# Square 32x32 tiles for s, full-height products with wq, and every B product inside U, in a 12-layer linear-attention kernel

## The reference

```python
for i in range(N_LAYER):                       # 12 layers, 16 heads of 8 channels
    qkv = x @ Wqkv[i].T + bqkv[i]
    q, k, v = jnp.split(qkv, 3, axis=-1)       # then reshaped to (B, H, T, D)
    att = jnp.einsum('bhqd,bhkd->bhqk', q, k) * scale
    y = jnp.einsum('bhqk,bhkd->bhqd', att, v)
    x = y.transpose(0, 2, 1, 3).reshape(B, T, C) @ Wproj[i].T + bproj[i] + x
# around it
x = _layernorm(x + _L0_attn_ref(x, ...))
x = _layernorm(x + _L0_ffn_ref(x, w_gate, w_up, w_down))
```

## Time and profile before

| | |
|---|---|
| median of 3 runs | 310.84 us |
| lowest and highest | 309.97, 310.84 us |
| the profiled execution | span 308.2 us from its first to its last instruction |
| TensorE matmul busy | 302.1 us, 98% |
| TensorE weight loads busy | 283.8 us, 92% |
| VectorE, ScalarE, GpSimd busy | 216.9, 192.0, 133.8 us |
| granted TensorE clock, mean | 0.999 |

### The profile page before, as it was taken

One profiled execution on the slowest core, in us unless ns is written; L12 is line 12 of the kernel. 1 busy time (PEld: TensorE's weight loads), 2 busy tenths in 40 slices (PEclk: granted clock), 3 DMA queues, 4 the chain that ended last, 5 costly groups with the idle time before them and its releaser, 6 DMA issues.

```text
span 308.2 us, 9599 instructions
## 1 busy us (share of the span) xinstructions
PE 302.1 (98%) x4010; PEld 283.8 (92%) x4010; DVE 216.9 (70%) x651; ACT 192.0 (62%) x459; POOL 133.8 (43%) x142
## 2 busy tenths in 40 slices
PE   8999999999999999999999999999999999999994
PEld 8989999899998998989989999899998889999983
DVE  0477586676876768758677587676765997888874
ACT  3458667686585675865758668577586276444451
POOL 3064180480723806418045072360634663655533
PEclk9999999999999999999999999999999999999999
DMA  7603003030030210300203002020000000121112
GB/s 265 265 2 113 6 6 109 4 113 2 2 115 3 74 43 4 113 4 10 105 5 113 2 3 79 4 75 6 5 0 2 2 2 0 37 64 41 34 35 72
DMA packets 8908, 14.96 MB, mean 49 GB/s; under 512 B 800, under 2 KB 5280, under 8 KB 8864
## 3 DMA queue, kind: packets, MB, share of 16 engines
q1 hardware_dynamic: 8144, 13.34, 13.1%
q10 hardware_dynamic: 720, 0.99, 0.9%
HBM read 12.23 MB, written 2.10 MB: 46 GB/s over the span
## 4 chain that ended last, share of the span: by engine, by line
PE 96%; DMA 1%; DVE 1%; POOLq 0%; issue 0%; POOL 0%; ACT 0%; SPq 0%
PE ps L988 14%; PE ps L1097 14%; PE ps L1063 13%; PE ps L1218 7%; PE ps L946 6%; PE ps L945 6%; PE ps L944 6%; PE ps L1027 4%; PE ps L1007 4%; PE ps L1206 4%; PE ps L1207 4%; PE ps L1178 2%; PE ps L1038 2%; PE ps L961 2%; PE ps L1014 2%; PE ps L999 2%
## 5 line engine op out<-in xcount | busy, mean ns | idle before, releaser
L428 POOL TENSOR_TENSOR wq_lo<-w,wq_hi 128x512 fp32r<-128x512 f32 x12 | 15.3, 1279 | 112.7 <-ACT wq_hi L551 112.7
L466 POOL TENSOR_TENSOR step_lo<-step,step_hi 128x512 fp32r<-128x512 f32 (+1 forms) x44 | 48.9, 1144 | 13.4 <-ACT step_hi L574 13.4
L944 PE MATMUL ps<-state_hi,step_hi 128*128 128x258 f32 x154 | 44.4, 288 | 0.0
L946 PE MATMUL ps<-state_hi,step_lo 128*128 128x258 f32 x154 | 43.6, 283 | 0.0
L945 PE MATMUL ps<-state_lo,step_hi 128*128 128x258 f32 x154 | 43.5, 282 | 0.0
L988 PE MATMUL ps<-w,gram 128*128 128x128 f32 x352 | 42.8, 275 | 0.0
L988 PEld LDWEIGHTS ps<-w,gram 128*128 128x128 f32 x352 | 41.9, 192 | 0.6
L547 ACT COPY gk<-ps 128x512 f32<-128x512 f32 x48 | 28.1, 586 | 21.3 <-PE ps L988 21.3
L1097 PE MATMUL ps<-step,gram 128*128 128x128 f32 x320 | 40.6, 281 | 0.0
L574 ACT CAST step_hi<-step 128x512 fp32r<-128x512 f32 (+1 forms) x44 | 24.7, 566 | 24.7 <-DVE step L764 24.7
L1097 PEld LDWEIGHTS ps<-step,gram 128*128 128x128 f32 x320 | 37.3, 192 | 1.3
(11 more groups left out here) (148 smaller groups left out, 671.2 us busy)
## 6 DMA issues: line engine op xcount, KB each, us to landing
w<-weights SPq DMA_DIRECT2D x12, 592.5 KB, 3.8
xchan<-x_chan SPq DMA_DIRECT2D x8, 256.0 KB, 4.0
out<-xchan SPq DMA_DIRECT2D x7, 256.0 KB, 2.3
xt<-x_tok SPq DMA_DIRECT2D x4, 258.0 KB, 5.5
xt<-x_tok ACTq DMA_DIRECT2D x3, 258.0 KB, 5.3
fw_int<-ffn_weights SPq DMA_DIRECT2D x1, 576.0 KB, 5.0
cst<-consts SPq DMA_DIRECT2D x1, 147.5 KB, 6.9
xt<-x_tok SPq DMA_DIRECT2D x1, 129.0 KB, 2.6
```

The lines of the kernel that those rows point to most:

```text
L466: nc.gpsimd.tensor_tensor(step_part(step_lo, g, True), step_part(step, g, True), step_part(step_hi_f, g, True), ALU.subtract).then_inc(ste ...
L944: nc.tensor.matmul(dst, l_hi, r_hi, start=True, stop=False)
L946: return nc.tensor.matmul(dst, l_lo, r_hi, start=False, stop=True)
```

## The change

The stages of TensorE's program get other shapes, and what fed them follows.

- `s_stage` becomes 64 matmuls of 32x32. Bank k of a half holds the pair of batches 2(4h+k) and the next, 128 rows by 256 columns. Row group i writes quarter (i + k) mod 4 of the partitions ("turned"), so one bank is written by four row groups, each in its own quarter. The weights wq are laid out by the host with the same turn, and `n_stage` contracts all 128 rows at once.
- `n_stage` has one product for each pair. In the first half, pairs 0 and 1 are plain f32, pair 2 takes three f32r passes with parts from VectorE (`s_third_hi`, `s_third_lo`), pair 3 takes three with parts from GpSimd. `n_done` counts pairs of banks now, not halves.
- `b_whole_stage`, `state_whole` and the special cases for the last two batches are gone; all 16 batches take `three_pass` in U.
- `step` is laid out by groups in order, so `step_part` is gone and the H loop takes one group after another.

```diff
                 def s_stage(h):
-                    for j in range(2):
-
-                        pe.wait_ge(m_ready, at(GROUPS, GROUPS if h else j + 1))
-                        for i in range(QUADS):
-                            r = slice(QUAD * i, QUAD * (i + 1))
-                            place = GB * (2 * h + j)
-                            last = nc.tensor.matmul(s_banks(h)[:, i, P * j:P * (j + 1)],
-                                                    mt[r, place:place + QUADS, :].rearrange("p b i -> p (b i)"),
-                                                    wp_cent[r, :] if last_layer else w[r, s, WP:WP + P],
-                                                    start=True, stop=True)
+                    pe.wait_ge(m_ready, at(GROUPS, GROUPS if h else 2))
+                    for j in range(2):
+                        for k in range(QUADS):
+                            b = 2 * (QUADS * h + k) + j
+                            for i in range(QUADS):
+                                own, r = slice(QUAD * i, QUAD * (i + 1)), QUAD * ((i + k) % QUADS)
+                                last = nc.tensor.matmul(ps[r:r + QUAD, HALF_BANKS[h].start + k, P * j:P * (j + 1)], mt[own, b, :],
+                                                        wp_cent[own, :] if last_layer else w[own, s, WP:WP + P],
+                                                        start=True, stop=True)
                     last.then_inc(s_done, 1)
...
-                def b_whole_stage():
...
                 def n_stage(h):
...
+                    for k in range(QUADS):
+                        turned = slice(P * k, P * (k + 1))
+                        out_k = n_bank(h, k)
+                        if h == 0 and k == 2:
+                            pe.wait_ge(wq_lo_ready, at(1, 1))
+                            pe.wait_ge(s_third_lo_ready, at(1, 1))
+                            last = three_pass(out_k, wq_hi[:, turned], wq_lo[:, turned], s_third_hi[:, :], s_third_lo[:, :])
+                        elif h == 0 and k < 2:
+                            pe.wait_ge(s_low_half_ready, at(2, k + 1))
+                            last = nc.tensor.matmul(out_k, w[:, s, WQ + P * k:WQ + P * (k + 1)], s_rows[:, k, :], start=True, stop=True)
+                        elif h == 0:
+                            pe.wait_ge(s_quad_hi_ready, at(1, 1))
+                            nc.tensor.matmul(out_k, wq_hi[:, turned], s_quad_hi[:, :], start=True, stop=False)
+                            pe.wait_ge(wq_lo_ready, at(1, 1))
+                            nc.tensor.matmul(out_k, wq_lo[:, turned], s_quad_hi[:, :], start=False, stop=False)
+                            pe.wait_ge(s_quad_lo_ready, at(1, 1))
+                            last = nc.tensor.matmul(out_k, wq_hi[:, turned], s_quad_lo[:, :], start=False, stop=True)
                         else:
...
+                            if k % 2 == 0:
+                                pe.wait_ge(s_lo_ready, at(2, k // 2 + 1))
+                            last = three_pass(out_k, wq_hi[:, turned], wq_lo[:, turned], s_hi[:, k, :], s_lo[:, k, :])
+                        if k % 2 == 1:
+                            last.then_inc(n_done, 1)
```

On VectorE and ScalarE, and in the host's layout:

```diff
                 def take_s():
                     dve.wait_ge(s_done, at(2, 1))
-                    nc.vector.tensor_copy(s_rows[:, 2:4, :], s_banks(0)[:, 2:4, :]).then_inc(s_high_half_ready, 1)
+                    nc.vector.tensor_copy(s_third_hi[:, :], s_banks(0)[:, 2, :]).then_inc(s_third_hi_ready, 1)
+                    nc.vector.tensor_copy(s_rows[:, 3, :], s_banks(0)[:, 3, :]).then_inc(s_high_half_ready, 1)
+                    dve.wait_ge(s_third_hi_ready, at(1, 1))
+                    nc.vector.tensor_tensor(s_third_lo[:, :], s_banks(0)[:, 2, :], s_third_hi[:].bitcast(F32),
+                                            ALU.subtract).then_inc(s_third_lo_ready, 1)
...
                 act.wait_ge(s_done, at(2, 1))
-                nc.scalar.copy(s_rows[:, 0:2, :], s_banks(0)[:, 0:2, :]).then_inc(s_low_half_ready, 1)
+                for i in range(2):
+                    nc.scalar.copy(s_rows[:, i, :], s_banks(0)[:, i, :]).then_inc(s_low_half_ready, 1)
                 act.wait_ge(s_done, at(2, 2))
-                nc.scalar.copy(s_hi[:, 0:2, :], s_banks(1)[:, 0:2, :]).then_inc(s_hi_ready, 1)
...
+                for i in range(0, QUADS, 2):
+                    nc.scalar.copy(s_hi[:, i:i + 2, :], s_banks(1)[:, i:i + 2, :]).then_inc(s_hi_ready, 1)
...
-        wts[:, :, WQ + P * r:WQ + P * (r + 1)] = np.tile(wqkv[:, QUAD * r:QUAD * (r + 1)], (1, QUADS, 1))
+        wts[:, :, WQ + P * r:WQ + P * (r + 1)] = np.roll(wqkv[:, 0:P], QUAD * r, axis=1)
```

More of the change, by code:

```diff
@@ L125, in build @@
         state_lo_f = state_lo[:].bitcast(F32)
-        state_whole = sb("state_whole", [P, WHOLE, P + 2])
-        b_whole = sb("b_whole", [P, WHOLE, P])
         step = sb("step", [P, BATCHES, P])
@@ L360, in n_banks, with n_bank @@
             return ps[:, HALF_BANKS[h], 2 * P:4 * P]
+        def n_bank(h, k):
+            return ps[:, HALF_BANKS[h].start + k, 2 * P:4 * P]
         def pair_banks(e):
@@ L465, in layer @@
                     pool.wait_ge(step_hi_ready, at(GROUPS, g + 1))
-                    nc.gpsimd.tensor_tensor(step_part(step_lo, g, True), step_part(step, g, True), step_part(step_hi_f, g, True),
+                    nc.gpsimd.tensor_tensor(group(step_lo, g), group(step, g), group(step_hi_f, g),
                                             ALU.subtract).then_inc(step_lo_ready, 1)
@@ L770, in layer @@
                 take_s()
-                if not first:
-                    for b in range(WHOLE):
-                        dve.wait_ge(b_whole_done, at(WHOLE, b + 1) - WHOLE)
-                        nc.vector.tensor_copy(b_whole[:, b, :], b_whole_out(b)).then_inc(b_whole_ready, 1)
                 low_of_s(0)
@@ L1080, in layer @@
                 s_stage(1)
-                if not first:
-                    b_whole_stage()
                 if last_layer:
@@ L1113, in layer @@
                     if e >= 4:
-                        pe.wait_ge(b_lo_ready, at(SPLIT_PAIRS, SPLIT_PAIRS + e - 3))
-                    if e == SPLIT_PAIRS:
-                        pe.wait_ge(h_whole_ready, at(1, 1))
+                        pe.wait_ge(b_lo_ready, at(PAIRS, PAIRS + e - 3))
                     for k in range(2):
                         b = 2 * e + k
-                        if b >= SPLIT:
-                            last = nc.tensor.matmul(ps[:, two.start + k, 0:P + 2], step[:, b, :], state_whole[:, b - SPLIT, :],
-                                                    start=True, stop=True)
-                            continue
                         last = three_pass(ps[:, two.start + k, 0:SCOLS], step_hi[:, b, :], step_lo[:, b, :],
@@ L1133, in a_stage @@
                 for b in range(GB * g, GB * (g + 1)):
-                    left = b_whole[:, b - SPLIT, :] if b >= SPLIT else bsum[:, b, :]
-                    last = nc.tensor.matmul(one_product(A_BANKS[g], b), left, step[:, b, :], start=True, stop=True)
+                    last = nc.tensor.matmul(one_product(A_BANKS[g], b), bsum[:, b, :], step[:, b, :], start=True, stop=True)
                 last.then_inc(a_done, 1)
```

122 lines of the change are left out of this document (33 added, 89 removed).

## The result

| | before | after |
|---|---|---|
| median | 310.46 us (4 runs) | 318.98 us (316.88 to 319.27) |
| profiled span | 308.2 us | 317.5 us (this execution: 319.27 us) |
| mean granted clock | 0.999 | 0.996 |

The change is **slower**: the ratio is 1.0254, 95% interval 1.0217 to 1.0291. I had forecast 307.3 us, and the range ended at 312.0. The median after is of four executions. One of them was disturbed (379.5 us at a granted clock of 0.754); the range and the ratio are of the other three.

What follows compares the result with a forecast made beforehand. The TensorE matmul stream and its waits were taken as the bound. A gain of 0.60 less 0.27 in U, 0.33 us in layers 1 to 10, plus 0.2 in layer 0, made 3.5 us: 310.84 to 307.3 us, range 304.6 to 312.0.

Steps and rivals of the forecast that it cites:

- number 1, s from square tiles: In `s_stage`, 64 matmuls of 32x32 run sixteen at a time, eight passes, 0.93 us (0.90 to 1.07).
- The issue can't feed the small tiles: Rival in `s_stage`: at 23 ns a record, 128 records take 2.94 us; slower, 328 us; chance 11%.
- The text on instructions: `s_stage` wants 256 instructions in 0.93 us, 3.6 ns each, left unpriced; a 16 KB code packet takes about 1.2 us.
- From the first matmul of s to N: Between `s_stage` and N, PE waits for ScalarE's first copy of 256 columns; N starts at about 118.13.
- The second half of N, set by GpSimd: In `n_stage`, PE waits for `s_quad_lo` from GpSimd; the second half starts at 120.02 instead of 120.41.
- H 4.56 us after s forecast: From N to H no change of tile shape is left; H starts at 121.45, effectively 122.05 before, gain 0.60 us.
- U of 48 passes of 0.12: In U, two f32 matmuls (0.45 us) become six f32r passes of 0.12, 0.72 us: a loss of 0.27.
- Layer 0: The first layer, without `b_whole_stage` before the change, gains 0.19 us instead of 0.33.
- Layer 11 and behind it: In the last layer GpSimd computes `bqp` first and delivers `s_quad_lo` at 240.20 as before: gain nothing.
- the first of the "wrong" ones: Sign in `s_stage` that would show the forecast wrong: starts more than 12 ns apart, or a group of four per 0.11 us.
- The collision of row groups: Rival in `s_stage`: four row groups writing one PSUM bank take turns, 3.5 us; slower, 335 us; chance 5%.
- The other two rivals: After `s_stage`, waits eat the gain, 310.8 us, 9%; or GpSimd isn't in the way of N, 304.8 us, 7%.

Runs made afterwards that it cites:

- run 9: The changed kernel with the square matmuls of `s_stage` over 64 moving columns instead of 128, all instructions kept: 316.47 us, ratio 1.019.
- run 2: The changed kernel with row group i of `s_stage` writing bank i of its half instead of bank k: 318.56 us, ratio 1.0258.
- run 1: The changed kernel with the old `s_stage` of 16 matmuls of 32x128, s then laid out wrongly: 307.21 us, ratio 0.990.
- runs 3 and 4: 32 one-column f32 matmuls (128 instructions) added between the first Gram matmuls, in the changed kernel (322.85 us) and in the kernel before (316.73 us).
- run 3: The changed kernel with 32 one-column f32 matmuls (128 instructions) added between the first Gram matmuls: 322.85 us, ratio 1.041.

## Why the prediction was wrong

**The step that failed is number 1, s from square tiles.** I priced the 128 records at eight passes of 0.112, 0.93 us to N, with 0.90 and 1.07 as ends. They take 1.84 where no block is late. The reading of the earlier trace rows was the error: `m_means` has 16 matmuls in 0.43 us, and I took this for the array's pace with room for a change of shape. It is 13 ns a record, and `s_stage` keeps just this, 12.9 (1.636 us over 127 intervals). Four times 0.43 was the plain answer, 1.7 us. I preferred a model of overlapping passes to the nearest row.

**The rival came closer.** "The issue can't feed the small tiles" named the place, and the point from which it decides, 12 ns a record. The stage runs at 12.9. Whether all of that is the issue stays open (run 9): 1.06 of the 1.64 us at most, and half the columns took 0.37 off, so the overlap of the array fell short as well. What was off is its price: at 23 ns a record I had 328 us, and 11% for it. At the pace of the earlier trace rows it would have been a loss of 0.45 us a layer against the forecast, some 312 or 313 us, just outside the range. It should have had a case of its own at this pace.

**The second half of the loss, 7.3 us, was in no case.** The text on instructions says that the stage uses up a 16 KB packet in 0.93 us while a packet takes about 1.2, and then leaves it there. The step missing was to ask what the whole dense part needs, 384 instructions, and how far ahead the blocks are fetched. The trace of before had it in the times of the packets against PE's count of instructions.

**The other steps held, but for the last layer**, by the run with the old `s_stage` (1):

- From the first matmul of s to N: 1.24 forecast, 1.22 measured (115.50, 116.72).
- The second half of N, set by GpSimd: 3.13 us after s forecast, 3.11 measured (118.61), and the pass with `s_quad_lo` came at 118.39, 0.23 after the one ahead of it, 0.11 late.
- H 4.56 us after s forecast, 4.54 measured (120.04), without a loss for a change of shape.
- U of 48 passes of 0.12. The layer: 19.67 forecast, 19.65 measured. The sum: 3.5 us forecast, 3.3 measured.
- Layer 0: 19.67 us against 19.86 before, 0.19 forecast and 0.18 measured.
- Layer 11 and behind it: nothing forecast, but from its `s_stage` to the end it is 71.8 us where it was 71.3, 0.5 lost. The first loss is a wait of 0.23 us for VectorE's `nu_part` (at 240.58), which the change itself doesn't have. So the spans differ by 3.0 us and not by 3.3.

Of the signs I had named, the first of the "wrong" ones came true, starts more than 12 ns apart. In the change itself N is set by PE, not by ScalarE (`s_rows` is there before 121.70), and the wait for GpSimd is gone because N starts later.

The collision of row groups (5%) is refuted by run 2, for tiles in different quarters of the partitions and at this pace. The Trainium skill (TensorEngine Tiling (Array Packing), Gotcha 1: PSUM Pressure) says that row tiles can't use one PSUM bank at the same time; no cost of it shows here, 318.98 us with one bank for four row groups and 318.56 with one for each. The other two rivals fall to run 1: the waits after s did not eat the gain, and GpSimd was in the way by 0.11 us.

**What stays open.** Why the packet of a block starts only some time after the block before it is entered, 0.3 to 1.6 us in most cases and once 4.4. Whether the pace of 16.6 ns a matmul is the issue, and why the array's work adds 0.15 us for sixteen tiles. And whether a version with all bits of s beats the kernel before: none that was run does. The one with upper halves in s (7) does, at 304.63 us; it gives up bits of s for that, and whoever takes it has to want that.

## What to carry to other kernels

Count instructions, not only array work. When small tiles multiply the number of matmuls, price the stage by the densest row of the same tile in the trace, in ns a record, and let no model of overlap undercut it. Then add up the instructions of the whole dense stretch around it: if more than 256 go by in the 3 us that a block took here, PE can stand still at block boundaries, in some repetitions of a loop and not in others, under the name "issue", with no engine to blame. Test a suspected block boundary with code that keeps the granted clock up: the tiny matmuls of runs 3 and 4 cost 3.6 and 6.2 us ahead of the first layer, and only part of it was their own time.

## What the hardware did that I had not expected

- PE's code arrives in blocks of 256 instructions, and a block could be used no sooner than 2.36 us after its packet had started (2.19 in the half-column version), though the packet itself takes 0.9 to 1.5 us. Nine standstills of 0.4 to 1.2 us came of it in the change, and the half-column version reached 1.9 us.
- Shifting the program by 128 instructions moves standstills from some layers to others. A change that only adds or removes instructions far ahead can so move the time of a stage it doesn't touch.
- Square f32 tiles of 32x32 over 128 columns pass at 0.42 us for sixteen, in any order of different tiles; with 64 columns at 0.31. Under it lies a pace of 4.15 ns an instruction, the same for both; that it is the issue is argued, not shown.
- Four row groups wrote one bank in four quarters of its partitions at no cost (318.98 us, and 318.56 with a bank for each).
- Behind 64 records of one-column matmuls the granted clock fell to its lower level for 3.4 us (run 3), and the Gram matmuls behind them ran at some 60% of their pace.
